# Causal attention on one Trainium2 core: even head groups go through the query blocks upwards, odd ones downwards, and every block's maxima are taken during the block before it

## The reference

```python
q = apply_rope((x @ W_q) ...)          # 16 heads of 16
k = apply_rope((lat @ W_uk) ...)       # lat: the normalised latent of x
v = (lat @ W_uv) ...
scores = jnp.einsum('bhqd,bhkd->bhqk', q, k) / jnp.sqrt(jnp.float32(HEAD_DIM))
scores = jnp.where(causal[None, None], scores, -jnp.inf)
attn = jax.nn.softmax(scores, axis=-1)
out = jnp.einsum('bhqk,bhkd->bhqd', attn, v)
```

## Time and profile before

| | |
|---|---|
| median of 3 runs | 6247.82 us (6246.75 to 6248.1) |
| span of the profiled execution | 6256.4 us, mean granted TensorE clock 0.936 |
| first DMA of the causal attention issued | 277.6 us |
| first score of the causal attention | 391.9 us |
| first DMA of the stage behind it issued | 2108.3 us |
| share of the span busy: PE, DVE, ACT | 91%, 76%, 59% |

### The profile page before, as it was taken

One profiled execution on the slowest core, in us unless ns is written; L12 is line 12 of the kernel. 1 busy time (PEld: TensorE's weight loads), 2 busy tenths in 40 slices (PEclk: granted clock), 3 DMA queues, 4 the chain that ended last, 5 costly groups with the idle time before them and its releaser, 6 DMA issues. The chain is left out here.

```text
span 6256.4 us, 100890 instructions
## 1 busy us (share of the span) xinstructions
PE 5666.6 (91%) x30906; PEld 2064.6 (33%) x30906; DVE 4785.9 (76%) x5974; ACT 3672.7 (59%) x7190; POOL 274.1 (4%) x330
## 2 busy tenths in 40 slices
PE   6489999999999588859999999999999999999776
PEld 5323333333333255542222222222222222222332
DVE  5387877777778788768888888887888888888724
ACT  2237677676676311234777777777777777777432
POOL 2300000000000000140000000000000000000201
PEclk7579999999999799877999999999999999999987
DMA  3402011020020000260200020000200002000000
GB/s 95 102 12 43 9 25 26 10 42 9 9 42 8 24 12 11 63 144 3 42 6 4 4 38 11 4 4 7 40 6 6 1 6 42 4 6 4 3 4 27
DMA packets 181757, 150.13 MB, mean 24 GB/s; under 512 B 28294, under 2 KB 168966, under 8 KB 177414
## 3 DMA queue, kind: packets, MB, share of 16 engines
q1 hardware_dynamic: 181254, 143.68, 11.1%
HBM read 96.67 MB, written 46.14 MB: 23 GB/s over the span
## 5 line engine op out<-in xcount | busy, mean ns | idle before, releaser
L862 DVE TENSOR_REDUCE att_mx<-ps 128x1 f32<-128x1024 f32 (+5 forms) x3463 | 3841.0, 1150 | 891.4 <-PE ps L740 816.4
L842 ACT ACTIVATE att_probs<-ps 128x512 f32<-128x512 f32 (+3 forms) x6400 | 3267.2, 590 | 1283.9 <-PE ps L780 1138.5
L740 PE MATMUL ps<-att_K,att_Q 96*128 96x512 bf16 (+2 forms) x6670 | 2025.3, 383 | 164.4 <-DVE att_mx L862 79.3
L780 PE MATMUL ps<-att_Q,att_K 99*128 99x512 bf16 (+3 forms) x6400 | 1978.2, 376 | 44.7 <-ACT att_probs L842 23.5
L806 PE MATMUL ps<-att_probs,att_V 128*32 128x512 f32 (+3 forms) x12800 | 1652.3, 592 | 0.0
L780 PEld LDWEIGHTS ps<-att_Q,att_K 99*128 99x128 bf16 x6400 | 521.4, 97 | 1897.2 <-ACT att_probs L842 1536.5
L740 PEld LDWEIGHTS ps<-att_K,att_Q 96*128 96x128 bf16 x6670 | 622.2, 98 | 804.5 <-DVE att_mx L862 289.5
L806 PEld LDWEIGHTS ps<-att_probs,att_V 128*32 128x32 f32 x12800 | 257.8, 108 | 623.0 <-ACT att_probs L842 557.6
L1119 PE MATMUL ps<-wguT,mlp_xqT 128*128 128x512 f32 (+1 forms) x384 | 170.8, 597 | 0.3 <-DVE mlp_h L1222 0.2
L822 ACT ACTIVATE att_negT<-ps 48x128 bf16<-48x128 bf16 x66 | 17.5, 265 | 241.6 <-PE ps L749 241.6
L1479 PE MATMUL ps<-xT_all,cn_w 128*128 x192 | 109.9, 737 | 27.7 <-DVE xT_all L1452 25.8
(11 more groups left out here) (210 smaller groups left out, 2896.8 us busy)
## 6 DMA issues: line engine op xcount, KB each, us to landing
att_K<-kT_scratch SPq DMA_DIRECT2D x60, 512.0 KB, 17.3
att_Q<-qT_scratch SPq DMA_DIRECT2D x408, 64.0 KB, 2.3
att_V<-v_scratch SPq DMA_DIRECT2D x10, 2048.0 KB, 36.3
v_scratch<-proj_vpad SPq DMA_DIRECT2D x32, 512.0 KB, 3.9
qT_scratch<-proj_partT SPq DMA_DIRECT2D x32, 384.0 KB, 3.4
kT_scratch<-proj_partT SPq DMA_DIRECT2D x32, 384.0 KB, 3.1
proj_x<-in_L_attn_x SPq DMA_DIRECT2D x16, 256.0 KB, 3.5
mlp_x<-in_L_attn_x SPq DMA_DIRECT2D x32, 128.0 KB, 2.0
```

The lines of the kernel that those rows point to most:

```text
L740: mm = pe.matmul(bank[:, 0:wide], Q[0:SROWS, slot_of(u), h, qt * P:(qt + 1) * P], K[0:SROWS, u // NQB, h, (c + m) * QB:(c + m) * QB + wide ...
L780: mm = pe.matmul(ring(at)[:, lo:QB], K[0:MROWS, u // NQB, h, kt * P:(kt + 1) * P], Q[0:MROWS, slot_of(u), h, lo:QB], start=True, stop=not ...
L842: act.activation(probs[:, (n_key[u] + kt) % 2, h, lo:QB], ring(at)[:, lo:QB], ACT.Exp, scale=SCALE).then_inc(emptied, 1)
L862: dve.tensor_reduce(mx[:, min(u % NQB, 1), h * QT + qt, c // 2:c // 2 + 1], flat[:, b * QB:b * QB + max_width(u, i)], AX.X, ALU.max).then_ ...
```

## The change

The order of the query blocks: before, every head group went from the 8-chunk block down to the 1-chunk one. Now the even groups go up from 1 to 8 chunks and the odd ones down from 8 to 1. Before, the 64 items of each group's first block were spread over the six last blocks of the group ahead (`EARLY`), and the six last blocks hosted no early items of the block after next. Now each block hosts the remaining items of the next block and, at its end, some of the block after next: the number in `ahead`, 14 steps' worth, held to the smaller of the two blocks' counts.

```diff
     def queries(u):
-        return NQB - 1 - u % NQB
+        return u if causal and u < NQB else NQB - 1 - u % NQB
...
     SEAM = 14
-    EARLY = 6 if causal else 1
-    ahead = [0 if causal and u % NQB >= NQB - EARLY else round(len(maxima((u + 2) % UNITS)) * SEAM / (keys(u) * GH))
-             for u in range(UNITS)]
-    hosted = [[((u + 1) % UNITS, i) for i in range(ahead[u - 1], len(maxima((u + 1) % UNITS)))
-               if (u + 1) % NQB or not causal] +
+    ahead = [round(min(len(maxima((u + 1) % UNITS)), len(maxima((u + 2) % UNITS))) * SEAM / (keys(u) * GH)) for u in range(UNITS)]
+    hosted = [[((u + 1) % UNITS, i) for i in range(ahead[u - 1], len(maxima((u + 1) % UNITS)))] +
               [((u + 2) % UNITS, i) for i in range(ahead[u])] for u in range(UNITS)]
-    for first in (0, NQB) if causal else ():
-        hosts = [(first - EARLY + e) % UNITS for e in range(EARLY)]
-        spare = [max(1, keys(h) * QB * 4.6 - sum(max_width(*it) + 64 for it in hosted[h])) for h in hosts]
-        items = list(range(len(maxima(first))))
-        given = 0
-        for e, h in enumerate(hosts):
-            upto = len(items) if e == EARLY - 1 else round(len(items) * sum(spare[:e + 1]) / sum(spare))
-            hosted[h] += [(first, i) for i in items[given:upto]]
-            given = upto
```

## The result

The changed kernel takes 6286.25 us (median of 4 runs, 6281.16 to 6291.3), the kernel before 6247.96 (median of 4, of which three lie between 6246.75 and 6248.1; the fourth, 18911.95, is left out of the ratio). The ratio is 1.0061 with a 95% interval of 1.0046 to 1.0076: slower by 0.6%. The forecast was 6242, within 6210 to 6277. It was wrong, and the change is slower where I had put 0.22.

What follows compares the result with a forecast made beforehand. PE and DVE were taken to hold each other up, PE waiting for free bank pairs. Two passes of 62.5 - 37.5 = +25 make +50, with the head's -55.5 that is -5.5: 6247.8 to 6242 us, range 6210 to 6277.

Steps and rivals of the forecast that it cites:

- the head: Start of the causal attention: 16 narrow reductions and 14 of the second block replace 64 wide ones, first score at 336.4, -55.5 us.
- the new wait: Second (2-chunk) block: PE stands some 25 us for queries behind the K and V load; 58 us instead of 24.1, +34 per pass.
- 0.76 us per us: Marginal price of DVE work in a block, from the old 7-chunk block against the mean of six other long ones.
- Ascending blocks: Blocks of 1 to 8 chunks going up, priced by the most alike old block: +62.5 us per pass with the 34, +55 to +70.
- the upper bound that the prediction names: Marginal price of DVE work in a block: at most DVE's full time; the lower bound is PE's own share, 0.36 to 0.4.
- a wait for queries that doesn't occur: Ascending 1-chunk block: queries for the third block come 5.5 us after its start, a loss of 3 to 4 us; block +3.
- Descending blocks: Blocks of 8 down to 1 chunks, hosting only the next block's maxima: -37.5 us per pass, -30 to -43.
- 8 chunks: 0.504 us of DVE work per step, near the old 7-chunk block: Descending 8-chunk block: DVE work per step likened to the old 7-chunk block's, so 87 us, -5.5.
- B: Rival: DVE bounds the ascending half, each block taking at least its DVE work over 0.83; +37 us, 6279; chance 0.17.
- A: Rival: PE alone counts, so ascending blocks cost some 12 us instead of 25 per pass; 6216; chance 0.20.
- C: Rival: the second block's stall isn't there; gain 25 us per pass more, 6192; chance 0.05.
- D: Rival: PE stays at 1.2 GHz after the stall for the rest of the block; +22 us, 6264; chance 0.08.

Runs made afterwards that it cites:

- joined pieces: Last one-chunk pieces of two heads share one reduction (288 per head group, not 320): 6200.78 us on the kernel before, 6178.35 on the changed kernel with the load moved.
- the first experiment: Changed kernel with the odd head group's K and V load issued in the even group's 5-chunk block instead of its 2-chunk block: 6249.31 us, ratio 0.9999.

## Why the prediction was wrong

The blocks of two passes were put at +50 us and took +84; the head and the new wait came out. What failed is the price of the hosted items: the prediction followed DVE's work alone, along one line of 0.76 us per us, and gave the number of items, each a handover between PE and DVE, nothing beyond the 0.15 us of the reduction itself.

*The head*: right, -53.4 against -55.5, with the queries landed in time and the turn where it was put.

*The new wait*: right in place and cause, and its total came out (+32.4 against +34) with some luck: PE stood 20.0 us and not 25, and the part after it was longer. Moving the load away gave 19 us a pass; so much of the 32 was stall. The rest is the block's own 31 us of DVE work.

*Ascending blocks*: the sum, +69.9 against +62.5, fails in two terms. The 4-chunk block was priced at +5.5 and cost +12.2, the largest miss of a single block. The forecast started from the old 6-chunk block and added 0.057 to 0.125 us per step for the denser mix, 4 to 8 us over the 64 steps; it took 12.5. That is over even DVE's full time, the upper bound that the prediction names, which is 10.7 us for the 11 items and 8600 columns more. What it left out is that PE's work and its waits for a free bank pair add up: against the old 6-chunk block, scaled to 64 steps, PE has 5.2 us more work and stands idle for 10.9 us instead of 3.5. The 1-chunk block was priced by a wait for queries that doesn't occur; it takes 22.2 us for 13.48 us of DVE work at a granted clock of 0.66. By the pairs of equal blocks above, where 7 us at half clock cost 2 to 3 us, its 15 us at half clock are worth some 5 (my estimate).

*Descending blocks*: here the larger error lies, -24.7 against -37.5. The step that failed is "8 chunks: 0.504 us of DVE work per step, near the old 7-chunk block". I read the 7-chunk block's 0.673 us per step as the price of few columns and drew a slope of 0.76 from it. It is also the block that hosts a 6-chunk row, in three full items. The rows showed it: blocks that host rows of an odd number of chunks (8, 6, 4, 2) stood at 0.727, 0.779, 0.784, 0.753 per step, those that host even ones (7, 5, 3) at 0.673, 0.743, 0.740. A narrow item costs a handover as a wide one does. It explains 3.2 of the 3.7 us by which the descending 8-chunk block was missed, and most of the 3.0 of the 6-chunk block. It doesn't explain the whole slope: with joined pieces the old 8-chunk block goes from 0.727 only to 0.72 per step, and the 7-chunk block stays at 0.67. The ascending 4-chunk block shows the narrow items at work: in this stretch of DVE's timeline in the changed kernel it reduces two items, a wide and a narrow one, waits 0.24 us, reduces one, waits 0.53, again and again (the bracket is the wait ahead of the row):

```profile
479.05 1.69 DVE L850 TENSOR_REDUCE att_mx<-ps 128x1 f32<-128x1024 f32 x2 [0.53 <-PE ps L728]
480.98 1.22 DVE L850 TENSOR_REDUCE att_mx<-ps 128x1 f32<-128x1024 f32 x1 [0.24 <-PE ps L728]
```

The joined pieces bear this out for the descending 8- and 6-chunk blocks, which with them come to the forecast values. Of the other 6 us, 4.4 are in the 4-, 3- and 2-chunk blocks: that DVE no longer counts there was right (halving its work changes them by 0.5 us at most), but the floor of PE was put some 1.5 us too low in each. The last 1-chunk block makes the other 2.0.

*Rivals*: B's time, 6279, was the nearest, and its condition was met (share 0.79 and 0.82 in the 4- and 6-chunk blocks). Its mechanism was not: the 5- and 7-chunk blocks stand at 0.85, and joined pieces reach 0.88. That its time came near the measured one is luck. A fails in the 4- and 6-chunk blocks, where most of the excess goes with DVE's work, and holds for two thirds of the 7-chunk block's excess. C is what the first experiment made, and the stall was there. D didn't happen: from 405.5 us on, 4.2 us after the restart, the clock is 1.00.

## What to carry to other kernels

When work is shifted between stretches of a loop, price it by the number of handovers between the engines as well as by its size, without taking the price of a handover as fixed (under 0.2 to 0.67 us here), and sort the rows of before by what each stretch hosts before drawing a slope through them. The 5 MB of K and V delayed the small transfers behind them on the queue by some 30 us, so the place of such a load has to be a stretch longer than that; when blocks change places, look first at which of them carries it. The reordering was worth nothing by itself (0.9999 without the stall), but the look at its blocks led to joining the narrow pieces, which with it gives 1.2% and alone 0.8%. Beside the joined pieces the reordering is thus worth 0.4%, and the two intervals don't overlap.

## What was not expected of the hardware

With six loads of 512 KB and one of 2048 KB just issued on its queue, SP's next DMA, of 64 KB, took 29.0 us to issue in the changed kernel and 29.3 to 31.3 elsewhere, and those behind it 0.43 each; in the run with the queries ahead the 4 KB placements of the maxima had to wait behind it. After the 20.0 us wait PE restarted at half clock and was at 1.00 some 4 us later (the half clock ended at 405.5), but in a 1-chunk block full of waits for DVE it averaged 0.66, and 0.52 in the 139 us block in which PE was shown busy 113 us. Most blocks of the same work repeat to 0.1 us between executions where the clock is 1.00 (the ascending 4-chunk block took 62.4 us in four of them); one stretch at half clock made a 4-chunk block 1.6 us longer.
